# A grouped convolution with per-pixel weights: kernel columns summed by TensorE in PSUM, and the first x fill issued from two queues

## The reference, cut to what matters

```
sel = softmax(conv1x1(v, coupler_w) + coupler_b)          # 8 weights a pixel
sel = sel / sel.sum(axis=1)
conv = conv3x3(v, w) + bias                               # w: 8 sets x 64 filters
return x + einsum('bschw,bshw->bchw', conv, sel)          # v = group_norm(x)
```

## Time and profile before

| | |
|---|---|
| median of 3 runs | 349.02 us (348.99 to 349.83) |
| the profiled execution | 348.88 us |
| its span in the trace | 346.8 us |
| PE busy | 328.6 us, 95% of the span |
| DVE busy | 286.2 us, 83% |
| POOL busy | 229.4 us, 66% |
| ACT busy | 93.8 us, 27% |

### The profile page before, as it was taken

How to read it: one execution, slowest core, us unless ns; L and a number is a source line. 1 busy time by engine, 2 the same in 40 slices (tenths; PEclk the granted TensorE clock), 3 DMA queues, 4 the chain that set the end, 5 groups by cost and what they waited for, 6 DMA issues and landing times.

```text
span 346.8 us, 5530 instructions
## 1 busy us (share of the span) xinstructions
PE 328.6 (95%) x1730; PEld 157.4 (45%) x1730; DVE 286.2 (83%) x503; ACT 93.8 (27%) x131; POOL 229.4 (66%) x329
## 2 busy tenths in 40 slices
PE   8959799989999999999999999999999999999993
PEld 8924234434444344444544344444544344444441
DVE  2789999888599799887699699987799687777776
ACT  1659111145521111155511111164411111111110
POOL 4420099999984667999874577999874389533343
PEclk9987699999999999999999999999999999999998
DMA  6534969704991199007990299008840397002002
GB/s 216 214 88 87 275 136 233 164 0 108 235 245 42 30 235 218 7 0 185 180 246 16 66 218 205 0 0 212 176 100 0 89 239 163 0 15 55 0 0 68
DMA packets 30226, 41.30 MB, mean 119 GB/s; under 512 B 2112, under 2 KB 23232, under 8 KB 29824
## 3 DMA queue, kind: packets, MB, share of 16 engines
q1 hardware_dynamic: 29328, 37.49, 46.1%
q10 hardware_dynamic: 880, 3.58, 3.5%
HBM read 11.97 MB, written 4.72 MB: 48 GB/s over the span
## 4 chain that ended last, share of the span: by engine, by line
PE 62%; DVE 20%; POOL 11%; issue 6%; DVEq 1%; POOLq 0%
PE pair L372 35%; PE pair L384 12%; PE pair L380 9%; PE w_bank L432 5%; DVE high L702 3%; DVE pair L701 3%; DVE pair L685 2%; POOL quarter L1001 2%; DVE pair L687 2%; POOL v_pts L975 2%; POOL x_res L994 1%; POOL v_tail L967 1%; DVE half L710 1%; POOL bias_part L989 1%; POOL mixed L1005 1%
## 5 line engine op out<-in xcount | busy, mean ns | idle before, releaser
L372 PE MATMUL pair<-w_head,op 128*128 128x512 f16 x864 | 236.4, 383 | 8.6 <-DMA op<-v_tail 4.0
L372 PEld LDWEIGHTS pair<-w_head,op 128*128 128x128 f16 x864 | 83.5, 99 | 114.0 <-DVE half L710 8.8
L384 PE MATMUL pair<-w_tail,op 128*128 128x512 f16 x288 | 110.1, 382 | 0.5 <-DVE w_tail L850 0.5
L529 ACT ACTIVATE m_sb<-pair 128x512 f32<-128x512 f32 x72 | 42.9, 596 | 224.6 <-PE pair L384 223.7
L1001 POOL TENSOR_TENSOR quarter<-half 128x256 f32<-128x256 f32 x71 | 52.7, 742 | 66.6 <-DVE half L710 66.4
L701 DVE TENSOR_TENSOR pair<-pair,sel_now 128x512 f32<-128x512 f32 x71 | 49.5, 697 | 36.4 <-PE pair L384 35.7
L710 DVE TENSOR_TENSOR half<-pair,high 128x512 f32<-128x512 f32 x71 | 49.1, 692 | 9.8 <-DVE high L702 0.5
L380 PE MATMUL pair<-w_tail,op_two 128*128 128x512 f16 x144 | 55.2, 384 | 0.0
L685 DVE TENSOR_TENSOR pair<-pair,m_sb 128x512 f32<-128x512 f32 x72 | 49.6, 689 | 0.0
L687 DVE TENSOR_TENSOR pair<-m_sb,pair 128x512 f32<-128x512 f32 x72 | 49.3, 685 | 0.0
L702 DVE TENSOR_TENSOR high<-pair,sel_now 128x512 f32<-128x512 f32 x71 | 48.3, 681 | 0.0
(11 more groups left out here) (96 smaller groups left out, 178.1 us busy)
## 6 DMA issues: line engine op xcount, KB each, us to landing
op<-v_head SPq DMA_DIRECT2D x14, 600.0 KB, 8.2
x_res<-x_pix SPq DMA_DIRECT2D x8, 576.0 KB, 6.2
op_two<-v_head SPq DMA_DIRECT2D x14, 300.0 KB, 9.2
op<-v_tail SPq DMA_DIRECT2D x14, 300.0 KB, 7.3
op<-v_head SPq DMA_DIRECT2D x14, 288.0 KB, 8.4
out<-y_out SPq DMA_DIRECT2D x7, 576.0 KB, 4.0
x_raw<-x ACTq DMA_DIRECT2D x3, 1152.0 KB, 11.0
w_raw<-weight SPq DMA_DIRECT2D x3, 768.0 KB, 8.5
```

The source lines that it names most:

```text
L372: nc.tensor.matmul(dst, op[b][:, 0, j, at + r * PW:at + r * PW + P], w_head[:, j, r, :], start=fresh and r == 0, stop=False, skip_group_ch ...
L384: return nc.tensor.matmul(dst, op[b][:, 1, j, at:at + P], w_tail[:, j, 0, :], start=False, stop=True, skip_group_check=True)
L529: act.activation(m1_sb[:, i % LOOK, :], pair[i % SETS_OF_BANKS][:, 0, :], ACT.Copy).then_inc(m1_copied, 1)
```

## The change

- `kernel_sum` and VectorE's `kernel_point1` go. TensorE makes point 1 of each kernel row: three fp32 matmuls of 512 columns with an identity matrix, accumulated in PSUM (rows 0 and 1 in the two halves of `pair[2]`, row 2 in the second half of `pair[1]`). They stand where 30 of the small fill matmuls were; for row 2, two of the three come after the matmuls of the bound.
- `kernel_point2` becomes one instruction per row: -2 times column 1 plus point 1, read from PSUM.
- The second set of fill matmuls falls from 30 small ones to none, the wide ones from 10 to 6.
- Two of the five transfers of the first fill are issued by ACT (`fill_beside`) and no longer by SP.
- The head of x's point 0, part 0, moves from ACT (after the last bound) to VectorE (`first_head`), and its tail goes ahead of `weight_bound`.
- ACT makes the heads of weight point 2 directly after those of point 1; VectorE makes both sets of weight tails ahead of `coupler_parts` and the later tails of x; the tails of weight point 3 come before `with_bias`, and `seed(0, 0)` before `less_maximum`.
- TensorE does three first points ahead of `w_heads[1]`, then two second ones, then the logits.
- GpSimd's last two raw points no longer wait for `w_heads[0]`.
- The matrices that are loaded grow from two to three (the identity).

```diff
-WARM_SMALL = (28, 30)
-WARM_WIDE = 10
+WARM_SMALL = 28
+WARM_WIDE = 6
...
+        w_pt1 = [pair[2][:, 0, :], pair[2][:, 1, :], pair[1][:, 1, :]]
...
-            warm_small(WARM_SMALL[1])
+            def kernel_point1(r, columns):
+
+                for kx in columns:
+                    last = nc.tensor.matmul(w_pt1[r], eye_mat[:, :], w_raw[:, r, kx, :], start=kx == 0, stop=kx == 1)
+                return last
+
+            pe.wait_ge(w_loaded[0], 16)
+            kernel_point1(0, (0, 2, 1)).then_inc(w_point1, 1)
+            pe.wait_ge(w_loaded[1], 16)
+            kernel_point1(1, (0, 2, 1)).then_inc(w_point1, 1)
+            pe.wait_ge(w_loaded[2], 16)
+            kernel_point1(2, (0,))
             pe.wait_ge(bounds_set, 2)
             pe.wait_ge(w_chain, 2)
             nc.tensor.matmul(w_bank[:, 0:2], ones[:, :], tiny[:, :], start=True, stop=False)
             nc.tensor.matmul(w_bank[:, 0:2], ones[:, :], w_max[:, :], start=False, stop=True).then_inc(w_added, 1)
+            kernel_point1(2, (2, 1)).then_inc(w_point1, 1)
...
+            for i in range(3):
+                first_point(i, 0, 0, i == 0)
             for i in range(2):
-                first_point(i, 0, 0, i == 0)
+                first_point(i, 1, 0, i == 0)
             pe.wait_ge(c_tails, 1)
-            pe.wait_ge(h_done, 1)
             pe.wait_ge(h_first, 2)
             pe.wait_ge(t_first, 2)
             logits(0)
-            for i in range(2):
-                first_point(i, 1, 0, i == 0)
-            first_points(2, 0)
+            first_point(2, 1, 0)
...
+            def fill_beside():
+
+                pts, cols = slice(0, 2), slice(0, PW + FIRST_PAIRS)
+                act.wait_ge(h_first, 2)
+                act.dma_start(op[0][0:C, 1, pts, cols], v_head[0:C, pts, cols]).then_inc(first_in[0], 16)
+                act.dma_start(op_two[0][C:P, :, cols],
+                              v_head[0:C, 1, cols].unsqueeze(1).to_broadcast([C, 2, PW + FIRST_PAIRS])).then_inc(first_in[0], 16)
+
             bound_of(0)
             first_heads(1, 0)
             bound_of(1)
             bound_of(2)
-            first_heads(0, 0)
+            fill_beside()
             act.wait_ge(w_chain, W_STEPS)
-            w_heads_of(0, slice(0, 1))
-            w_heads_of(0, slice(1, 2))
-            w_heads_of(0, slice(2, 3))
+            for r in range(K):
+                w_heads_of(0, slice(r, r + 1))
+            w_heads_of(1)
             first_heads(1, 1)
             first_heads(0, 1)
             first_heads(2, 0)
-            w_heads_of(1)
...
+            def kernel_point2(r):
+
+                dve.wait_ge(w_point1, r + 1)
+                if r == 2:
+                    dve.wait_ge(w_heads[0], K)
+                dve.scalar_tensor_tensor(w_pt2[:, r, :], w_raw[:, r, 1, :], -2.0, w_pt1[r], ALU.mult, ALU.add) \
+                    .then_inc(w_point2, 1)
...
+            def first_head():
+
+                dve.wait_ge(v_first[0], 1)
+                dve.wait_ge(h_first, 1)
+                dve.tensor_scalar(v_head[:, 0, PW:PW + FIRST_PAIRS], v_pts[:, 0, 0:FIRST_PAIRS], norm_scale[:, 0:1], None,
+                                  ALU.mult).then_inc(h_first, 1)
...
             input_tails_of(1, 0, 1)
-            kernel_sum(0)
-            kernel_point1(0)
+            first_head()
+            input_tails_of(0, 0, 2)
             first_input_point(1)
-            kernel_sum(1)
-            kernel_point1(1)
             weight_bound()
+            kernel_point2(0)
             scales()
-            input_tails_of(0, 0, 2)
-            kernel_sum(2)
-            kernel_point1(2)
+            kernel_point2(1)
+            first_point_tail(0)
+            first_point_tail(1)
+            kernel_point2(2)
+            first_point_tail(2)
+            second_point_tails()
             coupler_parts()
-            first_point_tails()
-            kernel_point2()
             input_tails_of(1, 1, 1)
             input_tails_of(0, 1, 2)
             input_tails_of(2, 0, 3)
-            second_point_tails()
             input_tails_of(3, 0, 4)
+            last_point_tails(2, 0)
+            last_point_tails(2, 1)
             with_bias(0)
             maximum(0)
+            seed(0, 0)
             less_maximum(0)
-            last_point_tails(2, 0)
-            last_point_tails(2, 1)
-            seed(0, 0)
             add_up(0)
...
             inverse_deviation(0)
-            pool.wait_ge(w_heads[0], 1)
             for k in range(2, NP):
                 raw_point(k, LOADS - 1)
```

More of the change, by code:

```diff
@@ L86, in program @@
         w_raw = sb("w_raw", [P, K, K, N])
-        w_sum = sb("w_sum", [P, K, N])
-        w_pts = sb("w_pts", [P, 2, K, N])
+        w_junk = sb("w_junk", [P, K, N])
+        w_pt2 = sb("w_pt2", [P, K, N])
         w_head = sb("w_head", [P, NP, K, N], F16)
@@ L107, in program @@
         bias_all = sb("bias_all", [P, C])
-        mats = sb("mats", [P, 2, P])
-        mean_mat, diff_mat = (mats[:, k, :] for k in range(2))
+        mats = sb("mats", [P, 3, P])
+        mean_mat, diff_mat, eye_mat = (mats[:, k, :] for k in range(3))
         minus_half = sb("minus_half", [P, 1])
@@ L166, in program @@
         w_added = sem("w_added")
-        w_sums = sem("w_sums")
         w_point1 = sem("w_point1")
@@ L281, in first_fill @@
                 sp.dma_start(op[0][0:C, 0, pts, cols], heads[:, :, cols]).then_inc(landed, 16)
-                sp.dma_start(op[0][0:C, 1, pts, cols], heads[:, :, cols]).then_inc(fifth, 16)
+                if g or part:
+                    sp.dma_start(op[0][0:C, 1, pts, cols], heads[:, :, cols]).then_inc(fifth, 16)
                 sp.dma_start(op[0][C:P, 1, pts, below], heads[:, :, above]).then_inc(landed, 16)
-                if g == 0:
+                if g == 0 and part == 0:
+                    pass
+                elif g == 0:
                     sp.dma_start(op_two[0][C:P, :, cols], v_head[0:C, 1, cols].unsqueeze(1).to_broadcast([C, 2, width])) \
@@ L434, in _ @@
             pe.wait_ge(ready, 1)
-            warm_small(WARM_SMALL[0])
+            warm_small(WARM_SMALL)
             pe.wait_ge(mats_loaded, 16)
             group_sums(0)
-            warm_small(WARM_SMALL[1])
+            def kernel_point1(r, columns):
[8 more added lines that the diff above has]
+            kernel_point1(2, (0,))
             pe.wait_ge(bounds_set, 2)
@@ L547, in w_heads_of @@
                 if k < 2:
[L548 to L551, removed]
+                    act.wait_ge((w_point1, w_point2)[k], rows.stop)
+                if k == 0 and rows.start < 2:
+                    act.wait_ge(w_point2, rows.stop)
+                src = (w_pt1[rows.start], w_pt2[:, :, :], w_raw[:, :, 0, :], w_raw[:, :, 2, :])[k]
+                dst = w_head[:, k, rows.start, :] if k == 0 else w_head[:, k, :, :]
+                act.activation(dst, src, ACT.Copy, scale=half_scale[:, 0:1] if k < 2 else scale[:, 0:1]).then_inc(w_heads[k], 1)
             def bound_of(r):
@@ L557, in bound_of @@
                     act.wait_ge(w_bounds, r)
-                act.activation(w_pts[0:C, 1, :, :], w_raw[0:C, r, :, :], ACT.Abs, accum_out=w_max_part[0:C, r:r + 1]) \
+                act.activation(w_junk[0:C, :, :], w_raw[0:C, r, :, :], ACT.Abs, accum_out=w_max_part[0:C, r:r + 1]) \
                     .then_inc(w_bounds, 1)
@@ L811, in _, with first_point_tail @@
             dve.memset(var_eps[:, :], 0.0).then_inc(half_done, SETS_OF_BANKS)
[L812 to L817, removed]
+            def first_point_tail(r):
+                lo, hi, slot = ((0, C, 0), (C, P, 0), (0, P, 1))[r]
+                dve.wait_ge(w_heads[0], r + 1)
+                dve.scalar_tensor_tensor(w_tail[lo:hi, 0, slot, :], w_pt1[r][lo:hi, :], half_scale[lo:hi, 0:1],
+                                         w_head[lo:hi, 0, r, :], ALU.mult, ALU.subtract).then_inc(w_tails, 1)
             def second_point_tails():
@@ L822, in second_point_tails @@
                 for r, lo, hi, k, slot in ((0, 0, C, 1, 0), (1, C, P, 1, 0), (2, C, P, 2, 1)):
-                    dve.scalar_tensor_tensor(w_tail[lo:hi, k, slot, :], w_pts[lo:hi, 1, r, :], half_scale[lo:hi, 0:1],
+                    dve.scalar_tensor_tensor(w_tail[lo:hi, k, slot, :], w_pt2[lo:hi, r, :], half_scale[lo:hi, 0:1],
                                              w_head[lo:hi, 1, r, :], ALU.mult, ALU.subtract).then_inc(w_tails, 1)
[L826 to L840, removed]
+            def kernel_point2(r):
[4 more added lines that the diff above has]
+                    .then_inc(w_point2, 1)
             def last_point_tails(k, part):
@@ L1084 @@
     eye = np.eye(P, dtype=np.float32)
-    matrices = np.stack([0.5 * same_group, eye - 0.5 * same_group], axis=1)
+    matrices = np.stack([0.5 * same_group, eye - 0.5 * same_group, eye], axis=1)
     host = {
```

## The result

The changed kernel takes **346.45 us** (median of 5 runs, 346.25 to 347.18) beside 348.99 us (348.90 to 349.83) for the kernel before on the same chip: 0.9929 of it, with an interval of 0.9918 to 0.994. That is faster, by 2.5 us, 0.7%, and clear of the 0.3% (1.05 us) that the prediction took as the least that can be told. Forecast were 346.7 us, a range of 345.7 to 348.8 and 70 in 100 for faster. The profiled execution took 346.29 us, with a span of 344.5.

The account below looks back on a forecast made before the run. VectorE's chain to the end of the selection was taken as the bound, with fixed TensorE work after it. Terms -2.0 and -0.3 gave -2.3: 346.6 us profiled, plus 0.14 for the median, 346.7; range 345.7 to 348.8.

Parts of the forecast that it names:

- Part 1: VectorE's stretch from behind the scales to add_up: from 17.68 to 15.65 us, 2.0 us less.
- (a): After the scales, VectorE waits for ScalarE's first weight head, covered by kernel_point2(1) up to 0.1 us.
- (b): kernel_point2(2) needs three weight heads, ready some 2.0 us after the scales; VectorE arrives at 2.2, so no wait.
- (c): second_point_tails wait for ScalarE's heads of weight point 2: 0.85 us of idle VectorE.
- (d): less_maximum directly before add_up exposes ScalarE's exponentials and two hops: 0.55 us of VectorE wait.
- Part 2: Stretch up to the scales: weight_bound starts at 17.1 to 17.2 instead of 17.44, 0.3 us less.
- The turns with GpSimd: Before weight_bound, GpSimd's two raw points contend with VectorE's points and tails of x: 1.0 us, bounds 0 and 1.6.
- Part 3: Hidden work (first fill, last fp32 matmuls, wide fill matmuls, logits, second fill): moves nothing at the end.
- Low clock or dear fp32: Rival: fp32 matmuls ahead of the bound cost 1.77 us each, deciding from 1.29 on; 353.4 us, 9 in 100.
- The clock takes the gain back: Rival: TensorE idles longer before the seeds, low clock slows 10 matmuls past the selection by 0.2 us each; 348.7, 12 in 100.
- The gain doesn't arrive: Rival: something in the first round, such as x's load or GpSimd's chain, keeps its time; 348.7 to 349.0, 7 in 100.
- GpSimd holds `norm_scale`: Rival: raw points delay norm_scale by up to 0.8 us and ScalarE behind it; 347.5, within the forecast's range, no separate chance.

Follow-up runs that it names:

- the version with three edits: Changed kernel with GpSimd's wait for the first weight head back, coupler_parts ahead of second_point_tails, less_maximum ahead of seed(0, 0): 346.78 us, ratio 0.9929.

## Why the prediction was right

- **The bound.** VectorE's way to the selection set the start of the steady part, and the rest was a fixed 301.5 us. Right, to 0.1 us.
- **Part 1**, from the scales to `add_up`: 15.65 forecast, 15.78 measured (18.53 to 34.31), from 17.68. Wait (a) 0.1 against 0.17, (b) none as forecast, (c) 0.85 against 0.98, (d) 0.55 against 0.51. `kernel_point2` was taken at 0.65 and took 0.61 (20.94 to 21.55, where the next instruction stands right behind it). The coupler gave back 0.53 of the 0.6. The run with the sums on VectorE shows that the removed adds are more than the whole gain, and those with the coupler and the softmax that (c) was a real loss and (d) one that the old order pays elsewhere.
- **Part 2**, up to the scales: 0.3 less forecast, 0.42 measured. The turns with GpSimd cost 0.8 against 1.0, `first_head` 0.51 against 0.6, a fp32 matmul 0.86 against 0.91. The price was taken from 128 columns in the earlier trace rows and was 5% too high. The prediction's estimate from the Trainium skill's four passes (FP8 and Floating Point Precision, "TensorE Precision Notes") was 0.85, and the trace agrees with it: 0.86. The statement that TensorE is level with VectorE was nearly so: 0.3 us of slack, found from two sides (turns taken away, matmuls added). One bound was reckoned wrong: at 1.14 a matmul the bound's matmuls would start at 18.7, and that is 1.0 later than their 17.72 before, not 1.2; the 1.2 is counted from `weight_bound`.
- **Part 3**, what is hidden: the two-queue fill moves nothing, as said. But the forecast had the last transfer land near 20, with the 2.9 us of the earlier trace rows. Issued at 17.29, it took 4.1 and landed at about 21.4, and from one queue it landed no later. So TensorE's first point still waits 0.40 for it. It is hidden all the same.
- **The rivals.** *Low clock or dear fp32*: excluded, 0.43 an instruction; above a price of 1.29 it would have decided, and three matmuls more did cost 2.2 us. *The clock takes the gain back*: the low clock is there (2.52 us of idling, then about 0.50 granted from 43.5 on), the price is nothing, since VectorE and GpSimd hold the first tiles, as the run with the clock kept up shows. The prediction's cushion of 0.68 us was read off a kernel whose TensorE was itself slow there, and its sign of being wrong, TensorE at 0.50 after the selection, came for some 3 us and meant nothing. *The gain doesn't arrive*: not here, but it is what befell the version with three edits, by way of a transfer in the first round. The prediction named x for the second pair and GpSimd, and not `x_res`, which is the nearest thing: before the change it was issued at 36.52, took 12.1 us and landed 0.4 us before GpSimd's addition at 49.02 took it. It didn't hold the gain because its issue moved up too, to 33.84 (landing at 45.3, addition at 46.69). The prediction had the tails that SP sends ahead of it 2.5 us earlier, but didn't look at `x_res`: in this it was right by luck. With three edits the wait for it was 2.26. *GpSimd holds `norm_scale`*: no, it started at 12.45, within what x's landing moves it.
- **The sum.** -2.3 was forecast and -2.32 read in absolute times. The medians differ by 2.54; of the 0.2 more, 0.14 is x's later landing in the profiled execution after (`norm_scale` 12.45 against 12.31).

The 1.1 us left lying were two orders: GpSimd's raw points beside x's points, and the coupler behind a wait that it could have filled.

## What to carry to other kernels

Take off the engine that is full, and separate what the offload is worth from what the new order costs: here 5.0 us won and 2.5 lost, with the sums put back right ahead of their readers. After each reordering list the places where a consumer now stands right behind a producer on another engine, and put independent work there, which was worth its full 0.7 us. A second queue for issues is no gain by itself: the last transfer was issued 1.04 us earlier and landed no earlier. And when the stretch ahead of a round shrinks, look at what the transfers that the round needs have to spare: 0.45 us won on VectorE became 1.4 us lost in the medians, behind a load that took 4 us longer.

## What the hardware did that was not expected

- A fp32 matmul of 512 columns is two instructions of 0.43 us each, with the weight loads hidden: 0.86 us, against 0.20 to 0.22 for one in fp16.
- Two GpSimd instructions of 1.05 us cost VectorE's three-operand instructions in SBUF 0.27 and 0.53 us, the second twice the first, in two different kernels (1.09 and 1.35; 1.10 and 1.36).
- The same transfer of 576 KB, issued at 33.48 and 33.51, took 9.4 and 13.7 us in two kernels that differ in one order on VectorE. The DMA engines' time was full in both, from 33 to 43 us, at 274 and 230 GB/s.
- Of two executions in which TensorE idled 2.52 us ahead of the steady part, one was granted 0.58 of the full clock in the next 3 us and the other 1.00.
